# Graph layer on one Trainium2 core: paired groups take their inputs through the permutation, and 24 groups are paired instead of 16

## The reference, cut to what matters

```python
h = jnp.maximum(_layernorm(x, axis=-1), 0.0)                 # 3125 nodes, 64 features
msg = concatenate([h[dst], edge_attr], axis=1)               # 53125 edges, dst sorted
m = relu(msg @ W1a.T + b1a)
m = m @ W1b.T + b1b
agg = segment_sum(m, src, 3125) / maximum(counts, 1)         # src is in random order
z = relu(concatenate([h, agg], axis=1) @ W2a.T + b2a) @ W2b.T + b2b
out = x + concatenate([z, h], axis=1) @ Wr.T + br
```

## Time and profile before

| | |
|---|---|
| time, median of three (range) | 522.39 us (520.93 to 524.32) |
| span of the profiled execution, first to last instruction | 518.3 us |
| between that span and the median | 4.1 us |
| busy: TensorE / VectorE / ScalarE / GpSimd | 431.0 / 298.0 / 285.0 / 356.1 us |
| mean granted TensorE clock | 0.906 |

### The profile page before, as it was taken

The page is one execution under the profiler, slowest core; times in us unless marked ns, Lnnn a source line. Parts: engine busy times, 40 slices in busy tenths (PEclk is TensorE's granted clock), DMA queues, the critical chain, the costliest instruction groups (busy, mean ns, idle before and its releaser), DMA issues.

```text
span 518.3 us, 9203 instructions
## 1 busy us (share of the span) xinstructions
PE 431.0 (83%) x3133; PEld 390.0 (75%) x3133; DVE 298.0 (57%) x825; ACT 285.0 (55%) x576; POOL 356.1 (69%) x406
## 2 busy tenths in 40 slices
PE   6655988899999999998689779845999787987795
PEld 4555777888796988878578778845998777987674
DVE  7868642534656657555425547414765537667884
ACT  3442957774787777786658378171633772100073
POOL 4777777777677777777777777777777777776000
PEclk9876696987999899988899889986999897999999
DMA  7998998553959477978553989996999997778631
GB/s 182 306 338 229 257 266 271 155 156 108 303 143 294 141 257 265 257 255 263 164 151 92 336 249 333 312 331 196 360 326 336 328 322 221 248 214 256 177 86 43
DMA packets 62319, 123.45 MB, mean 238 GB/s; under 512 B 9369, under 2 KB 33374, under 8 KB 62270
## 3 DMA queue, kind: packets, MB, share of 16 engines
q1 hardware_dynamic: 49598, 91.25, 59.0%
q0 software_dynamic: 12672, 31.58, 18.8%
HBM read 71.53 MB, written 51.25 MB: 237 GB/s over the span
## 4 chain that ended last, share of the span: by engine, by line
POOL 32%; PE 26%; DMA 13%; issue 13%; DVE 7%; ACT 5%; SPq 2%; POOLq 0%; ACTq 0%; DVEq 0%
POOL slots_dram L568 24%; PE bank L1261 10%; POOL pairs_dram L551 8%; DMA slots_dram<-pay,pos_i 7%; PE bank L1241 4%; PE bank L1270 4%; DMA dstb<-in_dst 4%; DVE oh L774 2%; DMA rows<-slots_dram 2%; ACT eo L1059 2%; SPq L475 1%; PE bank L1294 1%; PE bank L1291 1%; PE bank L1211 1%; PE bank L1362 1%
## 5 line engine op out<-in xcount | busy, mean ns | idle before, releaser
L568 POOL DMA_INDIRECT slots_dram<-pay,pos_i x300 | 289.0, 963 | 98.7 <-issue 89.6
L1261 PE MATMUL bank<-rows,oh 128*125 128x130 f32 x1100 | 139.5, 287 | 40.3 <-DVE oh L774 40.1
L1261 PEld LDWEIGHTS bank<-rows,oh 128*125 128x125 f32 x1100 | 133.3, 198 | 44.6 <-issue 43.4
L1059 ACT ACTIVATE eo<-dstb,minus_lane 64x256 f32<-64x256 int32 x190 | 85.1, 494 | 94.5 <-DMA dstb<-in_dst 79.8
L1241 PE MATMUL bank<-pw,eo 128*128 128x128 f32 x856 | 119.9, 299 | 3.5 <-ACT pay L1042 2.3
L1241 PEld LDWEIGHTS bank<-pw,eo 128*128 128x128 f32 x856 | 113.3, 213 | 11.4 <-issue 8.0
L774 DVE TENSOR_TENSOR oh<-bank,rows 128x1500 f32<-128x1500 f32 (+5 forms) x67 | 81.8, 1223 | 17.6 <-DMA rows<-slots_dram 10.4
L1270 PE MATMUL bank<-hid,xch 116*128 116x131 f32 (+1 forms) x512 | 68.3, 294 | 14.6 <-DVE xch L724 8.6
L1270 PEld LDWEIGHTS bank<-hid,xch 116*128 116x128 f32 (+1 forms) x512 | 65.3, 205 | 16.9 <-issue 9.9
L551 POOL DMA_INDIRECT pairs_dram<-pay,pos_c x64 | 61.5, 960 | 22.3 <-issue 18.0
L1064 ACT ACTIVATE eo<-eo,one 64x512 f32<-64x512 f32 x95 | 68.3, 719 | 3.1
(11 more groups left out here) (198 smaller groups left out, 376.7 us busy)
## 6 DMA issues: line engine op xcount, KB each, us to landing
rows<-slots_dram SPq DMA_DIRECT2D x24, 864.0 KB
dstb<-in_dst SPq DMA_DIRECT2D x54, 256.0 KB, 7.7
eo<-in_edges_T SPq DMA_DIRECT2D x54, 256.0 KB, 4.9
rows<-pairs_dram SPq DMA_DIRECT2D x12, 864.0 KB
slots_dram<-zeros SPq DMA_DIRECT2D x9, 756.0 KB, 9.2
slots_dram<-pay,pos_i POOLq DMA_INDIRECT x300
rows<-slots_dram SPq DMA_DIRECT2D x8, 432.0 KB
rows<-slots_dram SPq DMA_DIRECT2D x16, 216.0 KB
```

What stands on the lines that cost most here:

```text
L568: pool.indirect_dma_start(out=slots_dram[:, :], out_offset=bass.IndirectOffsetOnAxis(ap=pos_i[:, u, k:k + 1], axis=0), in_=pay[:, u, k, :] ...
L1059: last = A.activation(eo[p, g % EB, a * HB:(a + 1) * HB], dstb[p, g % DB // 2, a * HB:(a + 1) * HB], ACT.Square, bias=minus_lane[p, g // 2 ...
L1261: last = T.matmul(o[0:BN, v * SW:(v + 1) * SW], oh2[:, r % 2, n, :], rows[:, sum_no[r] % RR, n, 0:SW], start=(t == 0), stop=(t == TB[ph] - ...
```

## The change

1. **More paired groups.** `ORDER` becomes `"OOOO" + "CCO" * 4 + "CO" * 4 + "OOOO"`: 28 pairs, 12 of kind C (24 groups) and 16 of kind O, the last of which holds only two tiles. GpSimd issues 242 + 96 = 338 indirect DMAs.
2. **The inputs are permuted, not the hidden rows.** For a C group, `feats` holds edges on partitions: 64 edge features, loaded from a new row-major copy of the edge features (`edges_rows`, 116 partitions by 8 tiles of 64 f32, 256 bytes in a piece), and a one-hot of 62 destinations, the bucket mark and the slot number, which VectorE writes (`features`). In a perm round (two per group now) `feats` is stationary and `perm` (256 columns) moves; the result is the permuted, transposed input. ScalarE copies it to `moved`, `paired_hidden` multiplies it with `pwx` (131 columns: weights, mark, count, slot), and ScalarE's Relu of that goes straight to `pay2`. C groups need no `dstb`, no `eo` and no one-hot on ScalarE; VectorE makes `perm` for four tiles in one instruction with the constant row in PSUM.
3. **Order.** The perms of a C group stand behind that group itself. ccount and crank of a C pair now also stand between the groups of the C pair before. `places_due` defers the slot numbers of a C group to the next place.
4. **Regions.** The double rows are in three regions (5, 5 and 2 pairs) instead of one, the O rows in five instead of six; 575 tile matmuls in the sum rounds. The planner's shares are `OO=25, CO=12, OC=14, CC=2`.
5. `zh`, `tot`, `sbar` and others share storage; start-up gets further constants (`pwx`, `near_c`, `slots_near`), and `dst_cols` is loaded always.

```diff
-ORDER = "OOOO" + "CO" * 8 + "O" * 7
+ORDER = "OOOO" + "CCO" * 4 + "CO" * 4 + "OOOO"
...
-    PAIRS = [5, 5, 5, 2, 1, 1]
+    PAIRS = [5, 5, 2, 2, 2]
+    PAIRED = [5, 5, 2]
...
-    AFTER_PHASE = [4, 4, 4, 2, 1, 0, 4]
+    AFTER_PHASE = [4, 4, 2, 2, 0, 4, 3, 2]
...
-    ROUNDS_FROM, FULL_FROM, EARLY_SHARE, SHARE, C_SHARE, MOST = 7, 10, 10, 23, -8, 32
+    ROUNDS_FROM, FULL_FROM, EARLY_SHARE, MOST = 7, 10, 10, 32
+    SHARES = dict(OO=25, CO=12, OC=14, CC=2)
...
+        if g // 2 + 1 in C_PAIRS:
             after[g].append(len(rounds))
-            rounds.append(("ccount", C_PAIRS.index(g // 2 + 1), 0, 0))
+            rounds.append(("crank" if g % 2 else "ccount", C_PAIRS.index(g // 2 + 1), 0, 0))
+        if g in C_GROUPS:
+            for half in range(2):
+                after[g].append(len(rounds))
+                rounds.append(("perm", C_GROUPS.index(g), half, 0))
...
+            def load_paired_edges(c):
+                if c >= XR:
+                    sp.wait_ge(S["ag"], last_perm[c - XR] + 1)
+                sp.dma_start(feats[:, c % XR, :, edges_in(c)], edges_rows[c, 0:TILE_A, :].rearrange("p (k f) -> p k f", f=D)).then_inc(s_xe[c % XR], 16)
...
+            def features(c):
+                g, e, pair = C_GROUPS[c], ones_in(c), c // 2 % 2
+                lanes = slice(K * (c % 2), K * (c % 2) + K)
+                made_of = feats[:, c % XR]
+                if c >= XR:
+                    dve.wait_ge(S["ag"], last_perm[c - XR] + 1)
+                V.tensor_copy(made_of[:, :, e + SEEN], mark[0:TILE_A, g, :])
+                V.tensor_copy(made_of[:, :, e + SEEN + 1], dest_x[0:TILE_A, pair, lanes])
+                V.tensor_tensor(made_of[:, :, e:e + SEEN], marks_all[0:TILE_A, e:e + SEEN].unsqueeze(1).to_broadcast((TILE_A, K, SEEN)),
+                                dst_x[0:TILE_A, pair, lanes].unsqueeze(2).to_broadcast((TILE_A, K, SEEN)), ALU.is_equal).then_inc(S["xp"], 1)
...
-                for t in range(2):
-                    k = K * (c % 2) + 2 * u + t
-                    last = V.tensor_scalar(perm[:, n % PR, 256 * t:256 * t + 256], slot_no[0:TILE_A].rearrange("p h s -> p (h s)"),
-                                           slot_x[0:TILE_A, c // 2 % 2, k:k + 1], None, ALU.is_equal)
-                last.then_inc(S["ohp"], 1)
+                k = K * (c % 2) + 4 * half
+                V.tensor_tensor(perm[:, n % PR], slots_near[0:TILE_A].unsqueeze(1).to_broadcast((TILE_A, 4, 256)),
+                                slot_x[0:TILE_A, c // 2 % 2, k:k + 4].unsqueeze(2).to_broadcast((TILE_A, 4, 256)), ALU.is_equal).then_inc(S["ohp"], 1)
...
             def rounds_after(g):
                 for r in after[g]:
                     hots(r)
+                    if rounds[r][0] != "perm" or r in last_perm:
+                        places_due()
                     if r >= 1:
                         take(r - 1)
-                    if rounds[r][0] == "crank":
-                        take(r)
...
-                    for side in range(2):
-                        for t, n in enumerate((TILE_A, TILE_B)):
-                            last = T.matmul(o[:, side * HW:(side + 1) * HW], perm[0:n, perm_no[r] % PR, 256 * t + 128 * side:256 * t + 128 * side + 128],
-                                            hid[0:n, c % HR, 2 * u + t, 0:HW], start=(t == 0), stop=(t == 1), skip_group_check=True)
+                    for u in range(2):
+                        for t, lanes in enumerate((TILE_A, TILE_B)):
+                            last = T.matmul(o[:, 256 * u:256 * u + 256], feats[0:lanes, c % XR, 4 * half + 2 * u + t, :],
+                                            perm[0:lanes, n % PR, 2 * u + t, :], start=(t == 0), stop=(t == 1), skip_group_check=True)
```

More of the change, by code:

```diff
@@ L165, in gnn_layer @@
     round_of = {n: r for r, n in sum_no.items()}
-    first_round = [min(r for r, v in enumerate(rounds) if v[0] == "sum" and v[1] == ph) for ph in range(NPH + 1)]
-    last_perm = [rounds.index(("perm", c, UNITS - 1, 0)) for c in range(len(C_GROUPS))]
+    first_round = [min(r for r, v in enumerate(rounds) if v[0] == "sum" and v[1] == ph) for ph in range(NPH + NCP)]
+    perm_rounds = [[rounds.index(("perm", c, half, 0)) for half in range(2)] for c in range(len(C_GROUPS))]
+    last_perm = [halves[1] for halves in perm_rounds]
     def last_touch(r):
@@ L788, in take @@
                 if kind == "perm":
[L789 removed]
+                    return
                 if kind == "ccount":
@@ new lines, in copy_window, with relu @@
+                    return
+                n = O_GROUPS.index(g)
+                if n >= WB:
+                    act.wait_ge(S["H"], made(O_GROUPS[n - WB]))
+                p, blocks = node_half(n), blocks_of(g // 2)
+                A.copy(pw[p, n % WB, 0:blocks, :], bank[p, 7, 0:blocks * HID].rearrange("p (k h) -> p k h", h=HID)).then_inc(S["pc"], 1)
+            def relu(g):
+                n = O_GROUPS.index(g)
+                u = n % PB
+                if n >= PB:
+                    act.wait_ge(s_sc[u], scatters_of(u, n))
+                for half in range(PARTS[g]):
+                    part = PART0[g] + half
+                    k0, k1 = half * K // 2, min(KT[g], (half + 1) * K // 2)
+                    act.wait_ge(S["H"], part + 1)
+                    A.activation(pay[:, u, k0:k1, 0:HID], bank[:, part % HIDDEN_BANKS, 0:(k1 - k0) * HID].rearrange("p (k h) -> p k h", h=HID),
+                                 ACT.Relu).then_inc(S["ev"], 1)
@@ L1106, in _ @@
                     late_weights()
-                for r in after[g]:
-                    if rounds[r][0] == "perm":
-                        copy_unit(r)
-                if ACT_FROM <= g + EB < NG:
-                    onehot(g + EB)
+                if g + EB in O_GROUPS and O_GROUPS.index(g + EB) >= ACT_FROM:
+                    onehot(O_GROUPS.index(g + EB))
             def mean(q):
@@ new lines, in hidden, with paired_hidden @@
+                    last = T.matmul(bank[:, part % HIDDEN_BANKS, (k % 4) * HID:(k % 4 + 1) * HID], eo[:, u, k * 128:(k + 1) * 128],
+                                    pw[:, n % WB, a, :], start=True, stop=True, skip_group_check=True)
+                    if k % (K // 2) == K // 2 - 1 or k == KT[g] - 1:
+                        last.then_inc(S["H"], 1)
+            def paired_hidden(c, half):
+                g = C_GROUPS[c]
+                if c < 2 and half == 0:
+                    pe.wait_ge(s_wx[c], 16)
+                if half == 0:
+                    pe.wait_ge(S["pc"], g + 1)
+                n = perm_no[perm_rounds[c][half]]
+                pe.wait_ge(S["ep"], n + 1)
+                for u in (2 * half, 2 * half + 1):
+                    part = PART0[g] + u
+                    pe.wait_ge(S["ev"], part - HIDDEN_BANKS + 1)
+                    for side in range(2):
+                        first = 256 * (u % 2) + 128 * side
+                        last = T.matmul(bank[:, part % HIDDEN_BANKS, side * HW:(side + 1) * HW], moved[:, n % 2, first:first + 128], pwx[:, c % 2, u, :],
+                                        start=True, stop=True, skip_group_check=True)
+                    last.then_inc(S["H"], 1)
```

486 lines of the change are left out of this document (275 added, 211 removed).

## The result

The changed kernel takes 596.02 us (median of four runs, 592.66 to 597.26) against 522.77 us of the kernel before in the same session: ratio 1.141 (95% interval 1.134 to 1.148). Ratios compare the runs within 1.5% of each kernel's fastest; times in us are medians of all its runs. The forecast was 551 us in a range of 511 to 574: the sign and the mechanism were right, the size 45 us short. The profiled execution has a span of 590.7 us.

A forecast was written before the change was run, and what follows sets the result against it. GpSimd bounds the kernel before at 1.26 us a scatter; TensorE takes over in groups 8 to 45: 84 + 283 + 10 + 43.5 = 420.5. Scatters end at 510.4, span 546.5 with the tail, median 551 us; range 511 to 574.

The forecast's parts named there:

- (a): Groups 9, 15, 21, 27: VectorE's crank chain between a C group's two `perm` makes TensorE wait, 15 us, taken in full.
- (b): First group of a C pair behind a round: VectorE's take, `feats` and `perm` make TensorE wait, 7 us, taken in full.
- (c): Runs of C groups: ScalarE's O one-hots wait for late `dstb`, delaying its copy for TensorE; 15 us, half taken.
- (d): Groups 19, 25, 31, 35, 43: the second sum's one-hot waits behind the crank chain; 10 us, taken in full.
- (e): Group 40 behind a bare crank, 4.3 us, and 1.2 at three groups of the CO stretch; 8 us, half taken.
- The waits of 7% before: TensorE, groups 8 to 29 before: measured 10.2 us or 7% over the summed pieces, partly clock, partly waits; 10 us taken.
- Landing, loading and first one-hot of the tail 7: Stretch between the last scatter and the tail's first one-hot: forecast 7 us, against 11.2 before.
- Rival 1: New waits on TensorE are hidden and it just keeps up: 507 to 517 us, say 510; chance 0.14.
- rival 2: No difference that can be told: half of the chosen waits, 20 us, giving about 525 us; chance 0.13.
- Rival 3: `feats` loads in 256-byte pieces land slowly, 16 groups wait 2 us more: 583 us; chance 0.07.
- everything, 7% and 55 us: Upper case of the sum: all of the 7% and all 55 us of new TensorE waits, giving 572 us.

The follow-up runs named there:

- loads_c: Changed kernel with the `dstb` loads of O groups issued three groups earlier, nothing else moved; 587.6 us, ratio 1.129.
- eight_late: Changed kernel with eight C pairs in the order of before, `dstb` loads earlier, perms' one-hots ahead of takes, node rounds spread; 524.5 us, ratio 1.008.
- spread: The kernel perms with its 12 C pairs one by one (CO twelve times) instead of CCO and CO four times each; 574.4 us, ratio 1.102.
- perms: Changed kernel with `dstb` loads three groups earlier and VectorE making perms' one-hots ahead of the takes of ccount and crank; 580.7 us, ratio 1.103.
- late_b: The kernel perms with node rounds (h, z) spread at 5 a group up to group 16; 577.9 us, ratio 1.110.

## Why the prediction was wrong, by its own steps

**What held.** GpSimd was the bound before (its last scatters are 300 in the trace, not 302, which changes no term); 26 scatters fewer at 1.26 us each take 33 us off it; TensorE takes over from group 8. The perm matmul of 256 columns was taken at 0.44 us: at the full clock eight take 3.63 us, 0.45 each. A C group is hardly cheaper on TensorE than before. GpSimd's waits for `pos_c` were expected to be 40 us or more: 106.9. From the end of group 45 to that of group 54 TensorE needed 71 us, forecast some 70. The waits were where the working put them (measured: added up from TensorE's timeline between 82 and 455 us):

| wait on TensorE | worked | taken | measured |
|---|---|---|---|
| (a) crank between a C group's perms | 15 | 15 | 10.8 |
| (b) first group of a pair behind a round | 7 | 7 | 3.1 |
| (c) ScalarE behind `dstb`, CCO runs | 15 | 7.5 | 17.3 |
| (d) crank ahead of sums | 10 | 10 | 13.3 |
| ccount ahead of sums, groups 18, 30, 34 | none | none | 2.7 |
| (e) bare crank, CO stretch | 8 | 4 | 8.5 |
| ScalarE's copy of `pwx` ahead of a window | none | none | 3.5 |
| sum | 55 | 43.5 | 59.2 (59.3 by the windows) |

**What failed.** From 550.6 to 596.0 us are 45.4 us:

1. *"(c) and (e) hang on landing times, and I take half, 11.5."* They came in full, 25.7 us. (d) was too low (in the five groups that it names, six rounds waited 13.3 us), 6.2 us ahead of sums behind ccount and of windows had no term at all, and (a) and (b) were too high: together the waits were 15.8 us short. The halving had no row behind it. loads_c shows at the same time that such a wait gives only part back when removed (13 us of wait, 6 to 8 us of time).
2. *"The waits of 7% before: I take half, 10, as the rest is replaced by these."* This term was to hold the clock. TensorE's busy time in the stretch was 314.0 us against 283 of pieces at full clock, 31 us more: 21 us short, the largest miss. It is the clock's: over windows of 2 us, busy time times what the granted clock lacked of 1 adds up to 33 us, and start to start the perms took 103.8 us where 84.5 were priced, the paired hidden rows 51.5 instead of 45.1, all other pieces within 2 us of their price. The mean clock of 0.90 there is hardly below the 0.92 of the earlier trace rows, but a loss of clock is paid only where TensorE is the bound, and then in full. The price of the clock was therefore a term of its own, in the kernel in which TensorE leads, and no remainder of waits.
3. *"Landing, loading and first one-hot of the tail 7 (shorter than the 11.2 of before, because TensorE has fewer left-over rounds then)"*. From the end of group 45 to that of the last scatter it was 89.3 us, forecast 89.9: "from group 46 on GpSimd leads again" held for the scatters, but not for the end. Behind them it was 13.9 us to the first one-hot of the tail instead of 7. TensorE had fewer rounds left over (12, before 18), but its sums came on top of the 71 us that it needed for groups 46 to 54, and it was at them until 556.5 us. Together 103.2 us, forecast 96.9: 6.3 short.
4. The tail took 32.2 us instead of 29.1, and the median lies 5.3 us over the span instead of 4.1: 4.4 us. Group 8 started 2.1 us earlier than forecast.

15.8 + 21.0 + 6.3 + 4.4 - 2.1 = 45.4.

**The rivals.** Rival 1 (the waits are hidden) and rival 2 (half of them) fell with the ledger: idle time counts one for one. Rival 3 (slow `feats` loads) isn't borne out: in every wait ahead of a perm that the trace names, it was VectorE that TensorE waited for, never that load. No rival held the possibility that came true, my own mechanism at its full price with the clock beside it; "everything, 7% and 55 us" was 572, and the range ended there. The range was built from the terms as priced; its upper end should have had the clock of the stretch at full price.

**Where the 73 us are.** Number of paired groups, with the regions and shares that go with it: from eight_late to spread 50 us, less what the early node rounds cost there (by perms and late_b, nothing that can be told). Order of work around them on SyncE and VectorE: from the changed kernel to perms 15 us by the medians, 20 by the ratios. CCO runs instead of CO: nothing by the ratios, 6 us by the medians. The form itself: some 4 us, within 2 to 6. None of the versions beats the kernel before. At eight pairs the two engines are nearly level, and each pair more is paid for on TensorE.

## What to carry to other kernels

When two engines are nearly level, relieving one of them is worth only the distance to the other: price both for the whole length, the left-over work at the end included. When the other takes over, its clock and every small wait that cost nothing before are paid in full, so price them as terms of their own and halve none without a row. To hoist work ahead of a wait, look at what the hoisted instruction itself waits for: a perm's one-hot needed only SBUF data and gave its gain, a sum's one-hot needed a load and took the gain away.
